# Wide products dealt 5 and 7 to a step instead of 6 and 6 in a recurrence on one Trainium2 core

## The reference, cut to what matters

```python
xw = einsum('ntd,dh->nth', x, Wx) + b              # L1
h_next = tanh(xw_t + h_prev @ Wh)                  # 512 steps, one after the other
...
f = sigmoid(x @ W_f.T + b_f); i = sigmoid(x @ W_i.T + b_i)   # L2
c = x @ W_h.T + b_h
hidden = scan of (f / (f + i)), (i / (f + i)) * c
```

## Time and profile before

| | |
|---|---|
| runs | 1461.23, 1461.57, 1466.59 us |
| median of the runs | 1461.57 us |
| the profiled execution, its own time | 1462.22 us |
| span of the profiled execution | 1460.4 us |
| steps of blocks 1 to 14 | 1021.46 us of the span, 102.40 to 1123.86 |
| mean granted clock of TensorE | 0.989 |

### The profile page before, as it was taken

One profiled execution on the slowest core, in us unless ns is written; L12 is line 12 of the kernel. 1 busy time (PEld: TensorE's weight loads), 2 busy tenths in 40 slices (PEclk: granted clock), 3 DMA queues, 4 the chain that ended last, 5 costly groups with the idle time before them and its releaser, 6 DMA issues. The chain is left out here.

```text
span 1460.4 us, 49898 instructions
## 1 busy us (share of the span) xinstructions
PE 1424.0 (98%) x21213; PEld 1128.5 (77%) x21213; DVE 993.7 (68%) x2706; ACT 661.0 (45%) x2200; POOL 690.4 (47%) x555
## 2 busy tenths in 40 slices
PE   7889999999999999999999999999999998899998
PEld 6568888888888888888888888888887777577776
DVE  5445767676767676767676767676756679998894
ACT  4444454545454545454545454545444443333332
POOL 3442434343434343434343434343434436778774
PEclk9899999999999999999999999999999999999999
DMA  9750333333333333333333333333324557989994
GB/s 375 274 206 6 60 60 60 60 60 60 60 60 60 60 60 60 60 60 60 60 60 60 60 60 60 60 60 60 53 39 96 143 106 126 285 319 330 335 330 146
DMA packets 442337, 168.16 MB, mean 115 GB/s; under 512 B 406481, under 2 KB 409681, under 8 KB 438914
## 3 DMA queue, kind: packets, MB, share of 16 engines
q1 hardware_dynamic: 441584, 164.53, 44.6%
q10 hardware_dynamic: 530, 0.44, 0.1%
HBM read 96.78 MB, written 68.16 MB: 113 GB/s over the span
## 5 line engine op out<-in xcount | busy, mean ns | idle before, releaser
L464 PEld LDWEIGHTS recb<-hs,scanS 128*128 128x128 f16 x16384 | 444.2, 96 | 161.4 <-DVE hs L1278 157.4
L464 PE MATMUL recb<-hs,scanS 128*128 128x32 f16 x16384 | 494.8, 177 | 14.8 <-DVE hs L1278 11.9
L699 ACT ACTIVATE hs<-pre 128x64 f16<-128x64 f32 x512 | 132.1, 258 | 611.4 <-DVE pre L1269 609.5
L1269 DVE TENSOR_REDUCE pre<-recb 128x64 f32<-128x128 f32 x512 | 149.5, 292 | 339.6 <-PE recb L464 339.5
L1122 DVE RECIPROCAL gates<-gates 128x64 f32<-128x64 f32 (+1 forms) x484 | 257.9, 555 | 0.4
L951 POOL TENSOR_TENSOR xt<-xt,hbuf 128x512 f32<-128x512 f32 (+1 forms) x65 | 99.2, 1526 | 170.7 <-ACT hbuf L703 170.7
L939 POOL TENSOR_TENSOR x1lo<-xt,x1hi 128x512 fp32r<-128x512 f32 x64 | 82.7, 1294 | 185.7 <-ACT x1hi L709 185.7
L957 POOL TENSOR_TENSOR gates<-gates 128x512 f32<-128x512 f32 x62 | 80.0, 1290 | 168.0 <-DVE gates L1122 168.0
L1278 DVE TENSOR_TENSOR hs<-konst,hs 128x64 f16<-128x64 f32 x512 | 104.0, 203 | 70.6 <-ACT konst L700 70.6
L964 POOL TENSOR_TENSOR xt<-xt,pout 128x512 f32<-128x512 f32 x64 | 76.0, 1187 | 150.5 <-DVE pout L1148 150.5
L1158 DVE TENSOR_TENSOR recb<-xw,recb 128x128 f32<-128x128 f32 x512 | 146.1, 285 | 0.0
(11 more groups left out here) (225 smaller groups left out, 2756.6 us busy)
## 6 DMA issues: line engine op xcount, KB each, us to landing
xt<-in_x SPq DMA_DIRECT2D x64, 256.0 KB, 3.6
g_d<-gst SPq DMA_DIRECT2D x64, 256.0 KB, 3.8
n_d<-nst SPq DMA_DIRECT2D x64, 256.0 KB, 3.0
x_d<-xt SPq DMA_DIRECT2D x64, 256.0 KB, 3.1
out<-gates SPq DMA_DIRECT2D x63, 256.0 KB, 6.4
xt<-x_d SPq DMA_DIRECT2D x28, 512.0 KB, 4.8
stage<-in_w SPq DMA_DIRECT2D x11, 1024.0 KB, 6.6
xt<-g_d SPq DMA_DIRECT2D x14, 512.0 KB, 7.1
```

The source lines that it names most:

```text
L464: last = nc.tensor.matmul(sums[t % 2][:, m].rearrange("p a b -> p (a b)"), w[:, k, m * P:(m + 1) * P], hs[:, k].rearrange("p a b -> p (a b ...
L699: nc.scalar.activation(hs[:, :, 0, :], pre[t % 2][:], ACT.Tanh, scale=unscale).then_inc(s_h, 1)
L1269: nc.vector.tensor_reduce(pre[t % 2][:], sums[t % 2].rearrange("p c a b -> p c b a"), axis=AX.X, op=ALU.add).then_inc(s_pre, 1)
```

## The change

`upto(t)` is the number of wide products issued before step t: 0, 5, 12, 17, 24, ... Even steps now hold 5 wide products and odd steps 7. The product that moves is the sixth of each group (chunk k = 1, high weights with low activations). It goes from the even step to the front of the following odd one. In block 15 the shift by four steps leaves even steps even.

```diff
+            def upto(t):
+                return 2 * QUOTA * (t // 2) + (QUOTA - 1) * (t % 2)
...
                 for t in range(TS):
                     step(j, t)
                     if j + 1 < NBLK:
-                        for e in range(t * QUOTA, (t + 1) * QUOTA):
+                        for e in range(upto(t), upto(t + 1)):
                             group_part(e // GM, e % GM, e % GM + 1, j)
                     else:
-                        for e in range(max(C * GM, (t + AHEAD) * QUOTA), min(len(GROUPS) * GM, (t + AHEAD + 1) * QUOTA)):
+                        for e in range(max(C * GM, upto(t + AHEAD)), min(len(GROUPS) * GM, upto(t + AHEAD + 1))):
                             group_part(e // GM, e % GM, e % GM + 1, j)
```

## The result

| | before | changed |
|---|---|---|
| median | 1462.0 us | 1468.37 us |
| lowest and highest of 11 runs | 1460.64, 1466.59 | 1466.77, 1469.42 |
| profiled execution, span | 1460.4 | 1466.2 |
| blocks 1 to 14 | 1021.46 | 1027.56 |

What follows compares the result with a forecast made beforehand. TensorE was taken to bound every step, with 0.17 to 0.25 us of slack in the ring. Terms +3.9, +0.6 and +0.1 gave +4.6 on 1462.22, 1466.8, less 0.65 for the median: 1466.2 us, range 1459.8 to 1473.

Steps and rivals of the forecast that it cites:

- 119.9 us of idle loads: Weight loads of small products: 0.27 us in each of 448 steps while the last wide product streams, no wait.
- The ring alone: A step's chain through the state to the next small products, without wide products: 2.085 us with a reciprocal, 2.01 without.
- rival of a state that is cheap to wait for: Hand-over from state to small loads costs under 0.05 us, so waits vanish; chance counted in the quick rival's.
- Even steps with a reciprocal: Five-product steps in blocks 1 to 14: wait 0.015 to 0.055 us for the state and take 2.085.
- late reduce of item 5: VectorE's reduce in step 17, behind a shortened even step: perhaps 0.03 us late, hidden by the odd step's 0.40 slack.
- The sum, +4.6: All pairs: +3.9 us with a reciprocal, +0.6 without, +0.1 in block 15.
- quick and slow: TensorE's two step lengths with six wide products, 2.26 and 2.30 us, set by an underived timing pattern.
- After a wait the pattern starts anew: Odd step behind a waiting even step: mostly the 2.28 kind, so 2.51 us with seven wide products.
- The quick rival: TensorE settles on 2.26 spacing everywhere: -2.1 us together, 1459.5, no measurable change; chance 0.17.
- The slow rival: TensorE takes slow spacing everywhere, plus the waits: +10.9 us with block 15, 1472.5; chance 0.22.
- The clock: Short PE waits lower TensorE's clock once a block in 14 blocks: 1488 us; chance 0.01.
- The seventh product at 0.216: Odd step's added wide product at the skill's isolated figure: 0.011 us cheaper, sum +3.4 instead of +4.6.

Runs made afterwards that it cites:

- split66: Kernel before, 6 and 6 wide products, with the reciprocal of even steps cut into halves around the state: median 1466.95 us, ratio 1.0008.
- four_eight: Kernel before with 4 wide products in even steps and 8 in odd ones: 1515.49 us in a single run.
- plain_pairs: 5 and 7 only in the eight pairs of a block without a reciprocal in the even step, 6 and 6 elsewhere: median 1463.84 us, ratio 0.9982.
- split57: Changed kernel with the reciprocal of even steps cut into halves around the state: median 1464.95 us, ratio to the kernel before 0.9993.
- wide_order: Kernel before with wide products reordered within a chunk, low activations second and low weights third: pairs 4.587 us; timed again, ratio 0.9993.
- small_order: Kernel before with the 16 small products of the high weights first, then the 16 of the low ones: pairs 4.587 us.

## Why the prediction was right, point by point

- *TensorE bounds every step of the kernel before, and the 119.9 us of idle loads are no wait.* Shown by split66: a shorter ring moves nothing. The slack was 0.18 to 0.28 us over all steps where I had 0.17 to 0.25.
- *The ring alone takes 2.085 with a reciprocal and 2.01 without.* Changed kernel 2.085 to 2.087; four_eight 2.086 or 2.087, and 2.015 to 2.018. The rival of a state that is cheap to wait for falls too: the loads started 0.051 to 0.054 behind it.
- *Odd step 2.49 to 2.53, taken as 2.51.* Measured 2.511 to 2.523. Nothing waits there; the seventh product buys no time.
- *Even steps with a reciprocal wait, those without don't.* Right for all eight positions.
- *Nothing else is late* (side work, banks, transfers, SP and POOL queues). The stretch accounts for the loss. The reduce of VectorE starts 1.00 us behind the first small product in all 32 steps of a block, as before, so the late reduce of item 5 did not occur. Block 15 has 71.06 and 70.97 us up to its last step; as other traces have between 69.2 and 71.3 there, that can't tell my +0.1 from nothing.
- *The sum, +4.6.* The stretch gave +6.10 where I had +4.5. Two terms were mis-sized. Pairs without a reciprocal: I took the middle of quick and slow for the five products, 2.055, and 2.51, +0.005; they took 2.062 and 2.511, +0.013, which is 0.9 us over 113 pairs. Pairs with one: +0.035, and +0.042 was measured on average (0.038 to 0.049 by position), 0.7 us over 111 pairs. In that term I had the waiting step right (2.085) and missed that the odd step behind it is up to 0.013 longer than my 2.51. "After a wait the pattern starts anew", always as 2.28, was too simple.
- *What I did not see.* The kernel before has two lengths of its own. I had one run of 1466.59 beside two of 1461 and put it down as scatter; I also saw 2.30 in block 15 beside 2.26 and 2.30 in blocks 1 to 14, and did not ask whether blocks 1 to 14 could take the other length. My sum fits because the trace I read and 9 of the 11 runs it was compared with were of the short kind, and that is luck. The median of all 77 runs is 1464.4, 3.9 us under the changed kernel's 1468.37; that of the upper cluster is 0.6 under it.
- *The quick rival* (1459.5) fell: no kernel here has quick steps throughout. *The slow rival* (1472.5) fell as a whole, though the decisive length, odd steps over 2.52, was reached on average in one position (step 15, 2.523). *The clock* stayed at 1.00 in blocks 1 to 14, even in four_eight.
- *What would show it.* The stretch of 1025 to 1027 us was 1027.56, just outside. I said the waits would show as idle of matmuls ended by line 1278, 4 us or so. Wrong view: that idle stayed at 1.0, since the modelled ends cover it. It shows in the starts, and in the idle of the loads, +3.3.
- *The seventh product at 0.216*, the figure for an isolated product by the Trainium skill, page "TensorE: Matmul & The Clock Gate", section "Back-to-back issue gap", would have made the sum smaller (+3.4). The rows of the changed kernel have 0.23 and more between wide starts (719.20 to 719.51, then 1.16 for five to 720.67), so the trace doesn't agree here either.

## What to carry to other kernels

Where one engine bounds every step of a ring and fills each step to within a quarter of a microsecond of the ring's own length, dealing its filler unevenly gains nothing by slack: the long step wins no time, and a short step that falls to the ring costs its wait, 3.14 us here. That part is shown. The other 2.96 us are the distance of one spacing of TensorE (4.573) from another (4.560), and there the sign isn't general: against the 4.587 that the same products of the kernel before can also take, it would be a gain, and plain_pairs was 0.18% faster than the runs beside it. Put the shortest step where the least side work stands ahead of the state, and read waits of this size from the distance between starts, not from busy or idle time. And before an effect of half a percent is put down to an edit, look at whether the same kernel already has runs of both lengths, and count how many of each were drawn.

## What the runs showed of the hardware that was not expected

- TensorE's stream has lengths that don't add. The same 64 small and 12 wide products took 4.560 (before, split66), 4.573 (split57) or 4.587 us a pair (wide_order, small_order), each with no wait for a state, and each constant over 14 blocks but for the first pair or two. Pairs of 6 and 6 have two lengths with nothing changed on TensorE: the kernel before has 4.560 in blocks 1 to 14 and 4.587 in block 15, split66 4.560 in both. Pairs of 5 and 7 with no wait had 4.573 in both kernels where no step of such a pair waits (split57, plain_pairs). One extra small product made 4.607 of 4.560, a second one left it there.
- The difference lies between the starts of wide products: 0.226 to 0.227 in a quick step, 0.224 to 0.236 in others, with an extra 0.01 in some steps ahead of the second one (0.322 for 0.313) or behind the last one (0.239 for 0.230). What in TensorE makes it is open.
- With equal work and no wait, the longer of the two lengths costs 5.95 us here, 0.4%: about as much as the whole change.
